# Graph attention units: one shared ring of PSUM slots for scores and maxima, a bank of its own for the other jobs, and denominators sent ahead of stacking

## The reference, cut to what matters

```
for c in range(6):
    q = ew[c,0] * (nodes[in_q] @ We[eq] + be[eq])      # k and v alike, from other nodes
    o = mha(q, k, v, Wq[c], Wk[c], Wv[c], Wo[c])       # softmax(q k^T / sqrt(d)) v, 8 heads
    nodes[c] = act_w[c] * o + q
```

## Time and profile before

| | before |
|---|---|
| median of 3 runs | 3431.9 us (3427.04 to 3450.86) |
| the profiled execution, its time | 3439.62 us |
| its span, first to last instruction | 3437.8 us |
| TensorE / VectorE / ScalarE / GpSimd busy in the span | 89% / 70% / 63% / 11% |
| mean granted TensorE clock | 0.922 of full |

### The profile page before, as it was taken

One profiled execution on the slowest core, in us unless ns is written; L12 is line 12 of the kernel. 1 busy time (PEld: TensorE's weight loads), 2 busy tenths in 40 slices (PEclk: granted clock), 3 DMA queues, 4 the chain that ended last, 5 costly groups with the idle time before them and its releaser, 6 DMA issues. The chain is left out here.

```text
span 3437.8 us, 49190 instructions
## 1 busy us (share of the span) xinstructions
PE 3055.6 (89%) x19007; PEld 1349.5 (39%) x19007; DVE 2418.9 (70%) x3094; ACT 2157.1 (63%) x2695; POOL 390.2 (11%) x330
## 2 busy tenths in 40 slices
PE   5698989899388999999999999999999999999994
PEld 4355555556123333333333333333333333333331
DVE  6655555552268877778887787878887777888853
ACT  1155555556225777767777677777777767777783
POOL 0000000000100111111111110111111111111013
PEclk9699999999658999989999899999999999999997
DMA  6000000000432434334443344444434433443302
GB/s 164 16 11 11 16 4 23 1 20 5 109 83 55 102 88 88 77 85 83 103 103 92 82 81 93 92 82 104 102 89 83 82 85 81 104 100 88 66 21 82
DMA packets 144224, 245.09 MB, mean 71 GB/s; under 512 B 56482, under 2 KB 92726, under 8 KB 140918
## 3 DMA queue, kind: packets, MB, share of 16 engines
q1 hardware_dynamic: 143414, 239.85, 31.4%
q10 hardware_dynamic: 576, 2.10, 0.2%
HBM read 165.00 MB, written 74.10 MB: 70 GB/s over the span
## 5 line engine op out<-in xcount | busy, mean ns | idle before, releaser
L1435 ACT ACTIVATE pt_b<-ps_max 128x1024 f32<-128x1024 f32 x1516 | 1497.1, 1025 | 536.2 <-PE ps_max L1286 531.5
L1468 DVE TENSOR_REDUCE mx_b<-ps_pair 128x2 f32<-128x1024 f32 (+1 forms) x1032 | 1245.6, 1207 | 250.9 <-PE ps_pair L1272 244.3
L1322 PE MATMUL ps_ctx<-pt_b,vs 128*32 128x512 f32 x6144 | 868.8, 639 | 3.8 <-ACT c_b L1424 3.5
L1468 DVE TENSOR_REDUCE mx_b<-ps_misc 128x1 f32<-128x512 f32 x1032 | 707.1, 685 | 207.0 <-PE ps_misc L1272 190.8
L1286 PE MATMUL ps_max<-qs,ks 50*128 50x512 f32 x3032 | 836.0, 456 | 3.6 <-DMA qs<-mpart 3.1
L1272 PE MATMUL ps_pair<-ks,qs 48*128 48x512 f32 x2040 | 574.3, 486 | 128.0 <-DVE mx_b L1468 99.3
L1272 PE MATMUL ps_misc<-ks,qs 48*128 48x512 f32 x1032 | 490.9, 476 | 58.9 <-DVE mx_b L1468 52.3
L1286 PEld LDWEIGHTS ps_max<-qs,ks 50*128 50x128 f32 x3032 | 388.3, 196 | 363.2 <-ACT pt_b L1435 226.7
L1272 PEld LDWEIGHTS ps_pair<-ks,qs 48*128 48x128 f32 x2040 | 239.4, 197 | 455.0 <-DVE mx_b L1468 378.4
L1272 PEld LDWEIGHTS ps_misc<-ks,qs 48*128 48x128 f32 x1032 | 203.8, 197 | 418.3 <-DVE mx_b L1468 335.3
L775 ACT ACTIVATE pt<-ps_max,cb 128x512 f32<-128x512 f32 x342 | 215.7, 685 | 237.0 <-PE ps_max L652 181.1
(11 more groups left out here) (181 smaller groups left out, 2375.5 us busy)
## 6 DMA issues: line engine op xcount, KB each, us to landing
partd<-part SPq DMA_DIRECT2D x24, 2048.0 KB, 9.1
qs<-partd SPq DMA_DIRECT2D x288, 128.0 KB, 5.7
ks<-partd SPq DMA_DIRECT2D x288, 128.0 KB, 6.8
xq<-node SPq DMA_DIRECT2D x24, 512.0 KB, 3.8
xk<-node SPq DMA_DIRECT2D x24, 512.0 KB, 4.8
xv<-node SPq DMA_DIRECT2D x24, 512.0 KB, 5.5
xf<-node SPq DMA_DIRECT2D x24, 512.0 KB, 4.7
node<-nt_b SPq DMA_DIRECT2D x48, 256.0 KB, 2.2
```

The lines of the kernel that those rows point to most:

```text
L1322: ins = pe.matmul(psO[SLOT * i:SLOT * i + SLOT, :], vs[u % 2][:, kb, QUAD * (s // HALF_STEPS) + i], pt[:, (QUAD * S + i) % ENTRIES], start ...
L1435: act.activation(pt[:, e:e + 2].rearrange("p k n -> p (k n)"), at[:], ACT.Exp, scale=SCALE_B).then_inc(exp_done, 1)
L1468: nc.vector.tensor_reduce(mx2[:, at:at + n], (psP, psX)[p % 2][:, 0:CHUNK * n].rearrange("p (h n) -> p h n", h=n), AX.X, ALU.max).then_inc ...
```

## The change

Pieces of maxima all have two tiles now: 64 a unit, one behind each score round. One list, `RING`, holds score rounds and maxima pieces in TensorE's order, and the entry at place `i` uses slot `i % 3` of `psM[0]`, `psM[1]`, `psP`. It waits until the entry three places back has been read: by ScalarE's exp if that was a score round, by VectorE's reduction if that was a maxima piece (`slot_free`). Between score rounds of units 1 to 22 there is always one maxima piece, so maxima piece `r` follows the slot of score round `r - 1`, and score round `r` that of maxima piece `r - 2`. Asides no longer replace a round: they go to `psX` behind the context step of their round, each waiting for the aside before it (`misc_free`), at rounds 2, 7, 9, 11, 13, 16, 19, 23, 27 and 42. Context steps come at odd rounds, as they did with respect to scores. The reciprocal comes eight rounds after the copy, not nine. In SyncE's queue `rows_of(4u + 1)` moves ahead of `stack(u + 2, 0)`. The first, unlooped projections and maxima are laid out anew over the same banks.

```diff
-        PLAN = {2: ("turn", 0, 1), 8: ("output", -1, 0), 11: ("project", 2, 0), 14: ("project", 2, 1), 17: ("project", 2, 2),
-                20: ("project", 2, 3), 24: ("output", -1, 1), 30: ("values", 1, 0), 34: ("values", 1, 1), 50: ("turn", 1, 0)}
+        PLAN = {2: ("turn", 0, 1), 7: ("output", -1, 0), 9: ("project", 2, 0), 11: ("project", 2, 1), 13: ("project", 2, 2),
+                16: ("project", 2, 3), 19: ("output", -1, 1), 23: ("values", 1, 0), 27: ("values", 1, 1), 42: ("turn", 1, 0)}
...
-                SIZES.append(min(2 - len(SIZES) % 2, BLOCKS * (q + 1) - sum(SIZES)))
-        NM = len(SIZES)
+        NM = BLOCKS
...
+        RING = []
+        for u in range(UNITS):
+            for r in range(ROUNDS):
+                RING += [("score", u, r)] + [("maxima", *m) for m in pieces_at(u, r)]
+        AT = {what: i for i, what in enumerate(RING)}
...
+        def slot(*what):
+            if what in AT:
+                return (psM[0], psM[1], psP)[AT[what] % 3]
+            return (psM[1], psP)[what[2] % 2]
...
                     if u < LAST:
                         spread(NG * u)
+                    if u < LAST:
+                        rows_of(NG * u + 1)
                     if u < LAST - 1:
                         stack(u + 2, 0)
                     if u < LAST:
-                        rows_of(NG * u + 1)
                         spread(NG * u + 1)
...
+                def slot_free(*what):
+                    if what not in AT:
+                        if what[2] >= 2:
+                            pe.wait_ge(mx_done, what[2] - 1)
                         return
+                    at = AT[what] - 3
+                    if at < 0:
+                        pe.wait_ge(mx_done, AHEAD)
+                        pe.wait_ge(mt_copied, 1)
+                        return
+                    kind, w, k = RING[at]
                     if kind == "score":
-                        pe.wait_ge(exp_done, exps(w, k + 2))
+                        pe.wait_ge(exp_done, ROUNDS * w + k + 1)
+                    else:
+                        pe.wait_ge(mx_done, NM * w + k + 1)
...
+                    for r in range(ROUNDS):
+                        to = slot("score", u, r)
+                        slot_free("score", u, r)
+                        score(u, 2 * r, to[:, 0:CHUNK])
+                        score(u, 2 * r + 1, to[:, CHUNK:TOK]).then_inc(s_ready, 1)
+                        for m in pieces_at(u, r):
                             maxima(*m)
                         for S in steps_at(u, r):
                             contexts(S)
+                        for kind, w, k in aside(u, r):
+                            misc_free(kind, w, k)
+                            if kind == "turn":
+                                turn_maxima(w, k, psX)
...
-                        g = GROUP_ROUND.get(BASE[u] + r - 9)
+                        g = GROUP_ROUND.get(ROUNDS * u + r - 8)
                         if g is not None and g < NG * LAST:
                             inverse(g)
```

More of the change, by code:

```diff
@@ L1045, in graph @@
+        FIRST_PLAN = {**PLAN, 24: ("turn", 0, 1)}
         del FIRST_PLAN[2]
[L1046 to L1066, removed]
-                SIZES.append(min(2 - len(SIZES) % 2, BLOCKS * (q + 1) - sum(SIZES)))
-        NM = len(SIZES)
+        LAST_PLAN = {**PLAN, 56: ("output", 0, 0)}
+        ROUNDS = NS // 2
+        def aside(u, r):
+            kind, ahead, k = (FIRST_PLAN if u == 0 else LAST_PLAN if u == LAST else PLAN).get(r, (None, 0, 0))
+            return [(kind, u + ahead, k)] if kind and 0 <= u + ahead <= LAST else []
@@ L1069, in graph @@
+        NM = BLOCKS
         HALF_M = NM // 2
         AHEAD = HALF_M + 4
-        def exps(u, n):
-            return NS // 2 * u + (n + 1) // 2
[L1075 to L1085, removed]
@@ L1265, in maxima @@
                         pe.wait_ge(stacked[p // HALF_M], STACK * (w + 1))
[L1266 to L1270, removed]
+                    to = slot("maxima", w, p)
+                    slot_free("maxima", w, p)
+                    pair, qb, kc = p // (BLOCKS // 4), p // 2 % KB, p % 2
+                    for odd in range(2):
                         rows = slice(P // 2 * odd, P // 2 * odd + MROW_B)
-                        ins = pe.matmul((psP, psX)[p % 2][:, CHUNK * k:CHUNK * k + CHUNK],
+                        ins = pe.matmul(to[:, CHUNK * odd:CHUNK * odd + CHUNK],
                                         qs[w % 2][rows, pair, P * qb:P * qb + P],
@@ L1376, in _ @@
                     unit(u)
-                for S in range(steps_at(LAST, len(ROUND[LAST]) - 1).stop, UNIT_STEPS * UNITS):
+                for S in range(steps_at(LAST, ROUNDS - 1).stop, UNIT_STEPS * UNITS):
                     contexts(S)
-                pe.wait_ge(exp_done, exps(LAST, NS))
-                output(LAST, 1, psM[0][:, 0:CHUNK])
+                misc_free("output", LAST, 1)
+                output(LAST, 1, psX[:])
             @block.scalar
@@ L1426, in unit @@
                 def unit(u):
[L1427 to L1445, removed]
+                    for r in range(ROUNDS):
+                        before = UNIT_STEPS * u + r // 2 - ENTRIES // QUAD + 1
+                        if before > 0:
+                            act.wait_ge(pv_done, before)
+                        act.wait_ge(s_ready, ROUNDS * u + r + 1)
+                        e = (NS * u + 2 * r) % ENTRIES
+                        act.activation(pt[:, e:e + 2].rearrange("p k n -> p (k n)"), slot("score", u, r)[:], ACT.Exp,
+                                       scale=SCALE_B).then_inc(exp_done, 1)
+                        g = GROUP_ROUND.get(ROUNDS * u + r)
@@ L1446, in unit @@
                         if g is not None:
                             context_copy(g)
-                free = [psM[n % 2][:, CHUNK * (n // 2):CHUNK * (n // 2) + CHUNK] for n in range(PJ)]
+                        for kind, w, k in aside(u, r):
+                            if kind == "turn":
+                                turned_maxima(w, k, psX)
+                            elif kind == "values":
+                                values(w, k, psX[:])
+                            elif kind == "project":
+                                project(w, k, psX[:])
+                            else:
+                                output(w, k, psX[:])
```

95 lines of the change are left out of this document (42 added, 53 removed).

## The result

| | before | after |
|---|---|---|
| median of 4 runs | 3437.72 us (3427.04 to 3450.86) | 3709.62 us (3699.53 to 3715.1) |
| ratio after / before | | 1.0786, 95% interval 1.0738 to 1.0834 |
| span of the profiled execution | 3437.8 us | 3713.3 us |
| mean granted TensorE clock | 0.922 | 0.953 |

The account below looks back on a forecast made before the run. It took the order in which TensorE waits as the bound: after the change, a closed two-round loop of 98.9 us a unit plus 12.1 of asides, 111.0 against 99.75, adds 248 us to 3431.9: 3680 us, range 3530 to 3800.

Parts of the forecast that it names:

- The loop: Context step, scores, exp, waiting maxima pair, next context step: 3.09 us for two rounds, 98.9 us a unit before asides.
- Asides: Mostly at odd rounds, inside the loop: project +1.73 us, output +2.01, values +1.16; together 12.1 us a unit.
- The sum: Loop 98.9 plus asides 12.1: 111.0 us a unit against 99.75, +248 us over 22 units.
- rival C: TensorE's idle time in the loop lowers its clock too, adding 185 us: 3865 us; chance 0.13.
- Rows ahead of stacking: SyncE's queue: VectorE's wait for denominators goes, worth 2.8 us a unit and most of the low-clock stretches.
- Wide pieces: VectorE's reductions take 77.3 us for 81.4, 4 us a unit less, on an engine that isn't full.
- Ends: Units 0 and 23: the last stays, the first could gain or lose 20 us; nothing taken.
- A: Rival: evacuation by the PSUM readers is the bound and the change pays, 258 us less, 3174 us; chance 0.10.
- B: Rival: half the aside time falls into the loop and the removed stop pays: 3430 us within 1%; chance 0.05.

Follow-up runs that it names:

- e3: Changed kernel with each score round's exp done by two 128x512 instructions in place of one 128x1024: 3771.93 us.
- e2: Changed kernel with the context step issued ahead of the round's maxima pair instead of behind it: 3634.48 us.
- e1: Changed kernel with all asides at even rounds instead of odd ones: 3537.85 us.
- e5: Kernel before with one part of the change alone, the denominators' rows sent ahead of stacking: 3312.52 us, ratio 0.971.
- e6: Changed kernel with the denominators' rows put back behind stacking: 3709.6 us, ratio 1.0853 to the kernel before.
- e7: Changed kernel with two context steps back to back in every fourth round in place of one in every second: 3949.48 us.

## Why the prediction was right

It named 3680 us, from 3530 to 3800; 3709.62 us was measured, and the mechanism that it named is the one in the trace. Point by point:

- **The loop.** Links 0.99, 0.60, 1.02, 0.05, 0.43, sum 3.09. Measured in the rows above: 1.00, 0.60, 1.02, 0.06, 0.43, sum 3.11. The choice of 0.43 (a pair that had waited) over 0.33 was right. The wait itself is 0.71 us for some 0.8. e3 showed that a link's length goes into the period in full, e2 that the loop goes with the ring and not with the exp.
- **Asides.** Context steps in TensorE's timeline of the changed kernel, with an output and then a project between them:

```profile
2135.82 1.06 PE L1321 MATMUL ps_ctx<-pt_b,vs 128*32 128x512 f32 x8
...
2140.92 1.07 PE L1321 MATMUL ps_ctx<-pt_b,vs 128*32 128x512 f32 x8
...
2145.74 1.07 PE L1321 MATMUL ps_ctx<-pt_b,vs 128*32 128x512 f32 x8
```

They are 5.10 and 4.82 us apart, so 2.00 and 1.72 over 3.10, for 2.01 and 1.73. e1 showed the other half of the argument, that an even round costs less: 105.35 us a unit, for about 105 expected.
- **The sum.** 111.0 us a unit forecast, 112.83 measured, 40 us over 22 units. Most of it is clock: 65 us of the changed kernel's units after the first passed at the lower level, against 208 before; by the earlier trace rows, 20 us of that cost 8.4, so 27 us, an estimate. The forecast had left none. That is rival C in small; the rest of its 185 us didn't come. The other 13 us fit a period of 3.11 us for 3.09, 0.02 x 32 x 22 = 14. That the total is only 30 us off is in part luck, for the ends gave 12 back.
- **Rows ahead of stacking.** The stop went as said. The prediction counted 2.8 us a unit "and most of the low-clock stretches" and gave no price to the second; e5 measured 5.1 us in all, in the kernel where it counts. In the changed kernel e6 shows no effect that can be told from zero, which the prediction implied by summing the unit from the loop, but didn't say.
- **Wide pieces.** VectorE's busy time over 22 units went from 1765.75 to 1757.53 us, 0.4 us a unit and not 4. The 1.207 us of the earlier trace rows is the mean of two forms; a wide reduction alone took 1.219 us before and 1.225 after. The rest is put down, without a run for it, to more reductions back to back before the change, where neighbours overlap (two of 1.22 in 2.35 us, row of e2), which a sum of durations doesn't see. As the engine isn't the bound, this moved nothing.
- **Ends.** Unit 0 and the last came out 12 us shorter together; nothing was forecast, 20 allowed.
- **Rivals.** A needed a loop under 2.74 us, and the loop took 3.11. By the Trainium skill's page "TensorEngine Tiling (Array Packing)", "PSUM Bottleneck", the reading of PSUM may become the bottleneck once tiling has sped TensorE up. The trace doesn't agree for this kernel: VectorE is idle 29% and ScalarE 37% of the 22 units. B needed half-hidden asides: e1's plan is what would have given them, and even so the kernel is slower than before by 3.5%. C named the clock, and 27 us of its 185 came. The Trainium skill's page "TensorE: Matmul & The Clock Gate", "A second HAM failure mode: psum-queue depth-cycling", tells of a kernel whose clock swung as TensorE idled briefly between groups. This ring doesn't agree: it idles 0.71 us in every 3.10 us, and the mean granted clock of its units is 0.99. In e7 the clock did swing (0.87), but with less idle time, so these runs don't show its short idle spells to be the reason.
- **Readings of rows that were off.** The prediction says that the lower level follows a stop like that of the earlier trace rows, and that idle spells of 0.3 to 1 us every two rounds passed at the upper level in the second row. Behind the stop of the earlier trace rows itself the clock stayed up:

```profile
1700.00:1734.00 34.00, 30.61 (x204) 11.18 (x205) 28.54 (x34) 25.37 (x29) 4.29 (x4) 1.00 0.23 60
```

Of the 21 stops of TensorE of 1.7 to 3.3 us in these units of the kernel before, 16 were followed by the lower level and five were not. And in 1526 to 1546 us TensorE idled three times, for 0.56, 0.08 and 0.80 us, not every two rounds; so that row says little of a ring that idles in each period. That the clock stayed up in the ring was not shown beforehand.

## What to carry to other kernels

A ring of slots shared by two streams is as deep as its slots, not as its banks. Here an engine in order has a long step every four entries and the ring has three slots: the entry ahead of the step waits for the entry behind the last one, and step, matmul, reader and semaphore add up to a period. Other depths were not run. Go round each such loop with durations from the trace before summing engines; where a loop sets the pace, work costs by its place in the list (a round's shift of seven asides was worth 172 us), and a stall removed beside it was worth nothing that could be measured. Test the parts of a change one at a time: the two-line reorder in it alone makes this kernel 3% faster.

## What the runs showed of the hardware that was not expected

- An exp of 128x512 from PSUM took 0.60 us and two neighbours 1.09 us together, while a copy with a bias of the same shape took 0.69 and two 1.26, the price that I had put on e3. What differs is the bias and not the function: the exps of the first attention layer, which have a bias tensor (`cb`), took 0.685 us in the same trace, and the context copy, which has none, 0.60 (groups of the changed kernel, the whole span and 1600 to 3000 us):

```profile
L775 ACT ACTIVATE pt<-ps_max,cb 128x512 f32<-128x512 f32 x342 | 215.7, 685 | 237.3 <-PE ps_max L652 181.3
...
L1426 ACT ACTIVATE c_b<-ps_ctx 128x512 f32<-128x512 f32 x49 | 29.4, 601 | 26.0 <-PE ps_ctx L1321 26.0
```

- Removing a stop of 2.4 us a unit gave back 5.1 us: the mean granted clock over the same units rose from 0.95 to 0.99.
- More idle time doesn't mean a lower clock. The changed kernel's TensorE is busy 1965 of 2481 us at 0.99, that of the kernel before 2061 of 2194 us at 0.95: waits of 0.71 us in every period passed at the upper level, and 16 of 21 single stops of 1.7 to 3.3 us were followed by the lower one. But e7 stood at 0.87 with no idle spell over 1.38 us, idle for 17% of its units. What sets the two apart these runs don't show.
